# Decoder, experts sublayer: weights added up by transposes, key sums from three engines, all gelus ahead, and the second lane three recurrence states behind

## What is computed

```python
xn = _rmsnorm(x, norm_w)
q = (xn @ w_q.T).reshape(b, t, H, 2, DK)                # H = 8 heads
sim1 = jnp.einsum('bthd,hkd->bthk', q[..., 0, :], keys[:, :, 0, :])   # 32 keys
sim2 = jnp.einsum('bthd,hkd->bthk', q[..., 1, :], keys[:, :, 1, :])
s1, i1 = jax.lax.top_k(sim1, K)                         # K = 8
s2, i2 = jax.lax.top_k(sim2, K)
...
fs, pk = jax.lax.top_k(all_sc, K)                       # of the sums s1 + s2
hidden = jax.nn.gelu(jnp.einsum('btd,bthkd->bthk', xn, wd), approximate=False)
hidden = hidden * jax.nn.relu(fs)
return jnp.einsum('bthk,bthkd->btd', hidden, wu)
```

## Time and profile before

| | us |
|---|---|
| median of 3 runs | 1138.74 (1136.88 to 1139.37) |
| the profiled execution, its own time | 1138.65 |
| span of that execution, first to last instruction | 1136.9 |
| TensorE / VectorE / ScalarE / GpSimd busy | 848.4 / 817.0 / 700.6 / 292.5 |
| mean granted TensorE clock | 0.876 of full |

### The profile page before, as it was taken

The page is one execution under the profiler, slowest core; times in us unless marked ns, Lnnn a source line. Parts: engine busy times, 40 slices in busy tenths (PEclk is TensorE's granted clock), DMA queues, the critical chain, the costliest instruction groups (busy, mean ns, idle before and its releaser), DMA issues. The chain is left out here.

```text
span 1136.9 us, 12090 instructions
## 1 busy us (share of the span) xinstructions
PE 848.4 (75%) x3576; PEld 517.3 (45%) x3576; DVE 817.0 (72%) x1651; ACT 700.6 (62%) x2225; POOL 292.5 (26%) x170
## 2 busy tenths in 40 slices
PE   2657275999977489988976647599996757998883
PEld 1547143555546434354344623455554643435432
DVE  2168763888655689998976875488775559999993
ACT  1412537998378285956852153899748819586590
POOL 0022000888356200000002200188826520000000
PEclk9877576999989699999996758599998969999997
DMA  8100001232000100000000000132200000000000
GB/s 230 38 0 1 1 1 42 89 95 78 1 1 1 33 0 1 0 1 1 1 19 0 1 1 2 45 97 93 65 1 1 1 0 1 1 1 1 1 1 19
DMA packets 26812, 27.37 MB, mean 24 GB/s; under 512 B 7172, under 2 KB 17146, under 8 KB 26746
## 3 DMA queue, kind: packets, MB, share of 16 engines
q1 hardware_dynamic: 24776, 24.63, 7.5%
q10 hardware_dynamic: 1970, 1.97, 0.6%
HBM read 25.28 MB, written 1.31 MB: 23 GB/s over the span
## 5 line engine op out<-in xcount | busy, mean ns | idle before, releaser
L1573 POOL TENSOR_TENSOR rs<-ve,minus_half 128x4 f32<-128x4 f32 (+1 forms) x56 | 89.4, 1596 | 652.7 <-DVE ve L1217 584.3
L963 PE MATMUL ps<-mem,ident 128*128 128x512 f32 x512 | 230.9, 600 | 31.1 <-DVE mem L1542 30.5
L1177 ACT ACTIVATE mem<-mem 128x32 f32<-128x32 f32 x1024 | 217.8, 308 | 0.0
L1593 POOL TENSOR_TENSOR mem<-mem 128x1024 f32<-128x1024 f32 x64 | 150.9, 2361 | 118.3 <-DVE mem L1392 118.1
L1392 DVE TENSOR_TENSOR_SCAN mem<-mem,ps 128x1024 f32<-128x1024 f32 x64 | 145.9, 2285 | 45.2 <-PE ps L799 45.2
L995 ACT ACTIVATE mem<-ps 128x512 f32<-128x512 f32 (+6 forms) x96 | 59.9, 623 | 179.7 <-PE ps L969 59.3
L1542 DVE SCALAR_TENSOR_TENSOR mem<-mem 128x1024 f32<-128x1024 f32 x128 | 159.4, 1279 | 15.3 <-ACT mem L1177 13.8
L963 PEld LDWEIGHTS ps<-mem,ident 128*128 128x128 f32 x512 | 94.1, 190 | 166.8 <-issue 92.3
L806 PE MATMUL ps<-mem,ident 128*128 128x512 f32 x256 | 119.5, 593 | 0.0
L1145 ACT ACTIVATE mem<-ps,mem,rs 128x77 f32<-128x77 f32 x256 | 101.9, 444 | 18.6 <-DVE mem L1445 18.6
L1534 DVE TENSOR_TENSOR mem<-mem 128x1024 f32<-128x1024 f32 x96 | 113.0, 1218 | 0.3
(11 more groups left out here) (221 smaller groups left out, 1221.2 us busy)
## 6 DMA issues: line engine op xcount, KB each, us to landing
mem<-bc_rows SPq DMA_DIRECT2D x64, 256.0 KB, 3.2
mem<-in_x_dram SPq DMA_DIRECT2D x4, 256.0 KB, 3.5
out_dram<-x SPq DMA_DIRECT2D x4, 256.0 KB, 2.3
mem<-in_mask_BxSxS_ik_dram SPq DMA_DIRECT2D x4, 154.0 KB, 3.7
mem<-n_L_ffn_expert_down_dram SPq DMA_DIRECT2D x1, 512.0 KB
mem<-in_L_xattn_Wo_dram SPq DMA_DIRECT2D x1, 512.0 KB
mem<-in_L_xattn_Wv_dram ACTq DMA_DIRECT2D x1, 512.0 KB
a_q<-in_L_xattn_Wq_dram SPq DMA_DIRECT2D x1, 512.0 KB, 4.5
```

Of the source, the lines that this page charges most:

```text
L963: mm = pe.matmul(ps[:, j, :], ident[:], WH[s][:, h % WB, j * 512:(j + 1) * 512], start=(h == 0), stop=(h == PH - 1), skip_group_check=True)
L1177: ins = nc.scalar.activation(SVA[s][:, n % 2, i * NK:(i + 1) * NK], sims[:, 1, h, :], ACT.Identity, bias=sims[:, 0, h, i:i + 1])
L1573: nc.gpsimd.tensor_tensor(RS[s][0:rows, i * n:(i + 1) * n], VE[s][0:rows, i * n:(i + 1) * n], minus_half[0:rows, 0:n], ALU.pow)\
L1593: nc.gpsimd.tensor_tensor(HC[s][:, n % 2], (HS, TU)[n % 2][s][:], spread(CQ[s][:, n % 2, :], 1, DJ), ALU.mult)\
```

## The change

`LAG` becomes 17: in every queue lane 1's instructions stand 17 us of planned time behind lane 0's, and the half-step offsets in cross1 go. The planned times of the other sublayers stay; `PASS` becomes 528.

In the experts, all expert inputs are made transposed (experts down, tokens across, `p_downT` stationary), eight per lane for all 512 tokens, and go through gelu into `GT` before the first weights. A head's weights are added up transposed: eight transposes of 128 x 128 per head that accumulate in PSUM. The product then lies as the last multiplication needs it; its turn and copy go. The key sums of a tile's heads are shared out by `SUMS_BY`: D on VectorE, A on ScalarE, P on TensorE, as a product of the turned similarities (`SIMT`, 64 rows of a head's two halves) with a constant 0/1 pattern `key_pick`, in banks 2 and 3, from where ScalarE copies 1024 columns. Each lane has per tile 3 D, 3 or 4 P and 2 or 1 A. Thresholds get a slack of 2^-20 of the largest absolute key, for which VectorE has a reduction and an operation more. The pattern is made by GpSimd in the setup, stored in DRAM, and loaded once per pass into lane 0's arena. The next pass's x is loaded after two tiles of experts, where it was loaded before their first.

```diff
-    LAG = 0
+    LAG = 17.0
     WB = 4
     XT_TURNS = 6
-    ACT_HEADS = (4, 7)
+    SUMS_BY = [("PDPADPDA", "PDPADPDP"), ("PAPDPADD", "PAPDPDPD")]
+    SLACK = -2.0 ** -20
...
+        GT, WH, HWT, KEY_PICK, SIMT, SUMS, T8, TT, TH, TM = per_lane(
+            gt=(P, (EB, S), F32), wh=(P, (WB, NE), F32), hwT=(P, (EB, P), F32), pick=(P, (NK, NK), F32),
+            simT=(P, (2, PH // 2, P), F32), sums=(P, (PH, NC), F32), t8=(P, (2, PH, TOP), F32),
+            tt=(P, (PH, TOP), F32), th=(P, (2, PH), F32), tm=(P, (PH,), F32))
+        _, SIM = per_lane(front=(P, (11 * DJ * S + S,), F32), sim=(P, (NB, 2 * PH * NK), F32))
+        OS = R
...
+                sp.wait_ge(p_const, 2)
+                sp.dma_start(key_rows.rearrange("p (i j) -> p i j", i=NK), key_made).then_inc(p_hrow, 16)
+                sp.wait_ge(p_hrow, 17)
...
+                w.link(nc.gpsimd.memset(key_made, 0.0))
+                for q in range(4):
+                    ins = nc.gpsimd.affine_select(
+                        out=key_made, in_=key_made, compare_op=ALU.not_equal, fill=1.0, base=-q * NK,
+                        pattern=([[0, NK], [-1, NK]] if q % 2 else [[-1, NK], [0, NK]]), channel_multiplier=1)
+                    if q < 3:
+                        w.link(ins)
+                ins.then_inc(p_const, 1)
...
-            [(0, 344), (3, 352), (10, 357), (18, 397), (30, 402), (38, 442), (50, 447), (58, 487), (70, 492),
-             (78, 532), (90, 539), (94, 541), (95, 545)],
+            [(0, 344), (1000, 1344)],
         ]
-        PASS = 550
+        PASS = 528
+        TILE, HEAD, FIRST = 38.0, 4.75, 16.0
+        pairs = [[(6.5, "keys", 0, 0)] for s in range(LANES)]
+        for s in range(LANES):
+            for k in range(NB):
+                at = FIRST + TILE * k
+                pairs[s] += [(at + HEAD * h - 6, "sum", k, h) for h in range(PH) if SUMS_BY[s][k % 2][h] == "P"]
+                pairs[s] += [(at + TILE + 1.9, "out", k, 0)]
+                if k + 1 < NB:
+                    pairs[s] += [(at + 22, "keys", k + 1, 0)]
+            pairs[s].sort()
+        PAIR = [{use[1:]: n for n, use in enumerate(pairs[s])} for s in range(LANES)]
...
-                                sp.wait_ge(sg["x_ready"][s], (b - 1) * TURNS["x_ready"] + 5)
+                                sp.wait_ge(sg["wh_ready"][s], (b - 1) * TURNS["wh_ready"] + 2 * PH)
...
+                            if s == 0:
+                                yield PASS * b + clock(4, 5)
+                                w.reach(sg["x_ready"][s], 4)
+                                sp.dma_start(key_pick, key_rows.rearrange("p (i j) -> p i j", i=NK)).then_inc(p_toe, 16)
...
+                    def key_sums(k, h):
+
+                        pair("sum", k, h)
+                        if k == 0:
+                            w.reach(G("sim_sb", s), NB)
+                            if s == 0 and h == 0:
+                                pe.wait_ge(p_toe, 48 + 16 * b)
+                        rows = slice(h % 2 * 2 * NK, (h % 2 + 1) * 2 * NK)
+                        for half in range(2):
+                            mm = pe.matmul(ps[:, 2 + half, :], SIMT[s][rows, k % 2, h // 2, :],
+                                           key_pick[rows, half * (NK // 2):(half + 1) * (NK // 2), :]
+                                           .rearrange("p i j -> p (i j)"), start=True, stop=True)
+                        mm.then_inc(G("pair_full", s), 1)
...
+                    def expert_inputs(e):
+
+                        if e < 2:
+                            w.reach(G("sim_sb", s), e + 1)
+                        else:
+                            w.reach(G("g_sb", s), e - 1)
+                        pe.matmul(ps[:, e % 2, :], p_downT[:, e * P:(e + 1) * P], XT[s][:], start=True, stop=True)\
+                            .then_inc(G("z_ready", s), 1)
...
+                        for k in range(NB):
+                            for h in range(PH):
+                                yield FIRST + TILE * k + HEAD * h + 1.6
+                                w.next(G("wh_ready", s))
+                                if h == 0:
+                                    if k == 0:
+                                        w.reach(G("g_sb", s), EB)
+                                    else:
+                                        w.reach(G("hw_ready", s), k)
+                                for e in range(EB):
+                                    mm = pe.matmul(ps[:, e // 4, (e % 4) * P:(e % 4 + 1) * P],
+                                                   WH[s][:, (k * PH + h) % WB, e * P:(e + 1) * P], ident[:],
+                                                   start=(h == 0 and e % 4 == 0), stop=(h == PH - 1 and e % 4 == 3),
+                                                   is_transpose=True, skip_group_check=True)
+                                mm.then_inc(G("wh_used", s), 1)
...
-                        yield 18 + 20 * k
-                        w.next(G("hw_ready", s))
-                        for e in range(EB):
-                            mm = pe.transpose(ps[:, 2 + e // 4, (e % 4) * P:(e % 4 + 1) * P],
-                                              HW[s][:, e * P:(e + 1) * P], ident[:])
-                        mm.then_inc(G("turned", s), 1)
...
+                    def key_sums(k, h):
+
+                        n = k * PH + h
+                        pair("sum", k, h)
+                        if n >= WB:
+                            w.reach(G("wh_used", s), n - WB + 1)
+                        copy(WH[s][:, n % WB, :].rearrange("p (a b) -> p a b", a=2), ps[:, 2:4, :], G("pair_free", s))
...
+                    def own_sums():
+                        for k in range(NB):
+                            sims = SIM[s][:, k, :].rearrange("p (h a n) -> p a h n", a=2, h=PH)
+                            for h in range(PH):
+                                if SUMS_BY[s][k % 2][h] != "A":
+                                    continue
+                                n = k * PH + h
+                                for quarter in range(4):
+                                    yield max(FIRST - 8, FIRST + TILE * k + HEAD * h - 12) + 1.8 * quarter
+                                    if n >= WB and quarter == 0:
+                                        w.reach(G("wh_used", s), n - WB + 1)
+                                    for i in range(quarter * NK // 4, (quarter + 1) * NK // 4):
+                                        ins = nc.scalar.activation(WH[s][:, n % WB, i * NK:(i + 1) * NK],
+                                                                   sims[:, 1, h, :], ACT.Identity,
+                                                                   bias=sims[:, 0, h, i:i + 1])
+                                ins.then_inc(G("asum_ready", s), 1)
...
+                    def others():
+                        for e in range(EB):
+                            yield 7.6 + 0.9 * e
+                            w.next(G("z_ready", s))
+                            nc.scalar.activation(GT[s][:, e, :], ps[:, e % 2, :], ACT.Gelu).then_inc(G("g_sb", s), 1)
...
+                        nc.vector.tensor_reduce(TM[s][:], T8[s][:].rearrange("p a h r -> p h a r"), AX.XY, ALU.max,
+                                                apply_absolute_value=True)
...
+                        th = TH[s][:, k % 2, :]
+                        w.link(nc.vector.scalar_tensor_tensor(out=th, in0=TM[s][:], scalar=SLACK,
+                                                              in1=TT[s][:, :, TOP - 1], op0=ALU.mult, op1=ALU.add))
+                        w.link(nc.vector.tensor_scalar(th, th, 0.0, None, ALU.max))
+
+                    def weighted(k):
+
                         w.reach(G("wh_used", s), (k + 1) * PH)
-                        w.next(G("g_sb", s))
-                        nc.vector.tensor_tensor(HW[s][:], HW[s][:], ps[:, 0:2, :].rearrange("p a b -> p (a b)"),
-                                                ALU.mult).then_inc(G("hw_ready", s), 1)
-                        if k + 1 < NB:
-                            yield 19 + 20 * k
-                            thresholds(k + 1)
-                    yield 94
-                    w.next(G("eo_drained", s), NB)
+                        if k == 0:
+                            w.reach(G("g_sb", s), EB)
+                        else:
+                            w.reach(G("pair_free", s), PAIR[s]["out", k - 1, 0] + 1)
+                        nc.vector.tensor_tensor(
+                            HWT[s], ps[:, 0:2, :].rearrange("p a (b c) -> p (a b) c", c=P),
+                            GT[s][:, :, k * P:(k + 1) * P], ALU.mult).then_inc(G("hw_ready", s), 1)
...
+                    def weights():
+                        for k in range(NB):
+                            for h in range(PH):
+                                n = k * PH + h
+                                wh = WH[s][:, n % WB, :]
+                                yield FIRST + TILE * k + HEAD * h
```

(9 more changed lines are left out.)

262 lines of the change are left out of this document (133 added, 129 removed).

## The result

The changed kernel takes 1220.6 us (1220.3 to 1226.0) beside 1138.8 us for the kernel before: a ratio of 1.073, 95% interval 1.070 to 1.077. The profiled execution has a span of 1224.2 us, 87.3 more than before; it is the longest of four (1226.0 us, the others 1220.3 to 1220.7). The forecast was 1103 us and its range ended at 1140, so both are wrong, and in the wrong direction.

The account below looks back on a forecast made before the run. The experts were taken as bound by VectorE, TensorE close behind. Experts -40, lag +15, borders -14, table loads +4: 1136.9 became 1101.9 us of span, 1103 measured time; forecast 1085 to 1125 (0.52), wider range 1070 to 1140 (about 0.8).

Parts of the forecast that it names:

- The tile: Experts, one tile of both lanes: VectorE 41.1 to 35.0 us, TensorE 38.8 to 35.0; at 92% busy a 38 us tile.
- the prices that I had bounded: Experts' tile: eight accumulating transposes between 1.04 and 1.97 us, taken as 1.06; key reduction plus small operation 0.5 per lane.
- The start of the stage: Start of the experts: twelve more expert inputs and gelus, partly hidden in free time, cost 4 us per batch (0 to 10.8).
- -40: Experts in all: tiles -21.9, start +4, end -2, together -19.9 us per batch, -40 over both.
- The lag, "paid once, at the very end": Whole kernel: lane 1 running 17 us behind costs +15 us (12 to 17), only once, at the end.
- what an overlap gives back: Borders between stages: half the neighbouring busy times added, fullest engine taken; ceiling 20.3 us, 14 taken as gain.
- third rival: Lanes block each other in the queues: stages before the experts +25 us per batch, 1168 us (cases 1141 to 1168); chance 0.11.
- two signs: What would show lanes blocking each other before the experts: recurrence states over 5.9 us or a front over 110.
- The table loads: Recurrence: the lagging lane's exp and logarithm switches need two more loads per batch, +4 us in all (0 to 5).
- The moved loads and the setup: Next x and pattern loads arrive well before use; setup work runs beside ScalarE's: nothing, some 6 us without that cover.
- The clock: TensorE in the experts' tiles: by the trace the clock stays at 2.4 GHz despite transposes; by the skill's rule 1.2 GHz.
- fourth rival: Clock falls in the experts' tiles: TensorE 35 becomes 66 us a tile, 184 us more, about 1330 us; chance 0.02.

Follow-up runs that it names:

- The runs with four own heads: Changed kernel, lane 1 late only in the experts' tiles, each lane's first four key sums on VectorE: 1144.4 us, lag 12 1156.7; ScalarE's head later, inputs and gelus closer 1131.3.
- the nested runs: Changed kernel with the lag starting ever earlier, always to the experts' end: from the experts 1172.7 us, from cross1 1185.1, from the scan 1210.7; everywhere 1220.6.
- the fastest kernel: Changed kernel, lag 17 only in the experts' tiles, first four key sums on VectorE, ScalarE's head one place later, inputs and gelus closer: 1131.3 us, ratio 0.993.
- the one with three engines: Changed kernel with its lag taken out (LAG = 0, cross1's half step back), key sums still shared over VectorE, ScalarE and TensorE: 1178.6 us, ratio 1.035.

## Why the prediction was wrong

*The tile: right, step by step.* VectorE 35.0 was forecast, 35.3 measured; TensorE 35.0 and 33.7; the cycle 38, 38.4 in the mean, at 92% of VectorE. ScalarE was low by 3.3 (29.2, 32.5 measured) and covered. Groups of the kernel after, 431 to 612 us (busy us, mean ns), with the prices that I had bounded:

```profile
L1043 PE MATMUL ps<-ident,mem 128*128 128x128 f32 x496 | 65.4, 284 | 11.4 <-DVE mem L1671 11.3
...
L1623 DVE TENSOR_REDUCE mem<-mem 128x8 f32<-128x128 f32 x7 | 2.0, 286 | 0.2
L1629 DVE SCALAR_TENSOR_TENSOR mem<-mem 128x8 f32<-128x8 f32 x8 | 1.4, 173 | 0.3
```

The small operations are 0.29 + 0.17 for the 0.50 assumed per lane. Eight accumulating transposes take 1.04 us at the full clock (row at 452.76 of the timeline; 1.06 assumed). What I didn't see is that the 38 us need the lag: side by side the same instructions make tiles of 44.2. I had put the gain of the tiles and the lag into the sum as two terms that don't touch, so the 38 was right by luck in part.

*The start of the stage: the step that failed first.* I charged it 4 us a batch, by free time of the engines (0 to 10.8), and "four weight buffers let VectorE go ahead". They didn't: the first heads were given to TensorE and ScalarE, whose queues hold 16 inputs and 16 gelus there. It measured +19 side by side and +23 to +31 with the lag. Free time was the wrong measure, twice over. The added inputs and gelus weren't hidden (11.3 us with the sums divided as before), and where the first heads stand in the queues cost 7.9 more. The runs with four own heads show the second part from the other side: with five instead of three of the first tile's heads on VectorE, and lane 1 late only from there on, the start is 57.0. Hence the experts were +22.5 us in two passes, not -40, and some +16 by estimate (twice the 8.0 of pass 1) in an execution whose two passes are alike.

*The lag, "paid once, at the very end": half right.* Lane 1 ends 14.3 us after lane 0 (12 to 17 forecast). But each border costs as well. I took half of the neighbouring busy times for what an overlap gives back (14 us). They give nothing and cost 48, as the nested runs show, and 12.3 more at the border out of the experts, where I had 3.3 as the most to be gained. So the sum missed the span by 122.3 us: 62.5 in the experts, 62.1 in the stages before them (52.1 for -14 + 4), and -2.3 at the end. This is the third rival's mechanism in its main point, that lanes block each other in the queues, and its 25 us per batch before the experts was well sized (22.3 and 29.8 measured). Where it looked for them is another matter: of its two signs, states over 5.9 us didn't come and a front over 110 did in pass 2 (114.7), and 29.8 of the 52.1 us are in cross1, which it didn't name. Its total of 1168 failed on the -40, which I had kept in it: 1136.9 + 22.5 + 52.1 + 12.7 = 1224.2. I gave it 0.11 because I asked only what the steady states do under a lag. That was zero, as I said (ten scans take 28.2 us after, as before in the middle of the stage), though it holds for a lag of three whole states and not for one and a half. The borders I had only tested for busy time.

*The table loads: right.* Four more, 5.1 us; both switches of the recurrence are there four times instead of twice:

```profile
L1150 ACT ACT_TABLE_LOAD x4 | 5.1, 1283 | 0.1
L1159 ACT ACT_TABLE_LOAD x4 | 5.1, 1283 | 0.1
```

*The moved loads and the setup: right.* The setup's last work ends at 42.1 us instead of 41.4, and the longer list of waits names a DMA only within the setup.

*The clock: the rows were right.* In the full tile, with sixteen times eight transposes, the granted clock is 1.00. The fourth rival doesn't happen. The rule of the Trainium skill ("TensorE: Matmul & The Clock Gate", Part 4: PE-mode transpose) that transposes don't engage the full clock is contradicted by the earlier trace rows, where TensorE had hardly anything but transposes at 0.51 and the clock then stood at 0.99; this tile doesn't test it, since the heads' transposes are 16.2 of its 33.7 busy us and the rest are matmuls of other kinds. The clock falls elsewhere, in the starts and at the borders (0.77, 0.70).

## What to carry to other kernels

Where engines take their work in a fixed order, price an added operation by what stands behind it in its queue and who waits for that, not by the engine's free time. An engine that is moved off the critical work for balance must keep it at the start of a stage, until the others have caught up: here the first four heads on VectorE, with one more exchange in the order, took 8 us off the start of each pass. A lag between lanes pays in the stage whose order is made for it, and opening and closing it costs as well, since a lane alone is bound by its own chain: open it in as few stages as possible, and count the border behind the last one.

## What was not expected of the hardware

One thing, and it is of the queues and the clock together. Four key-sum matmuls take 1.98 us at the full clock and 3.78 at the low one, and the low one comes in the very 45 us in which the engines wait for one another (granted clock 0.77). Where most of those waits are gone the clock is high again. Windows of the fastest kernel, from its first key sum to its first weighted product:

```profile
408.80:444.60 35.80, 32.57 (x145) 19.90 (x144) 30.43 (x61) 26.12 (x82) 0.00 (x0) 0.95 0.00 1
```

Over its whole span the mean granted clock is 0.884 in this execution of 1127.2 us and 0.869 in the three of 1131.3 to 1132.0; over that of the changed kernel it is 0.845. The mean by itself doesn't rank kernels: with the sums divided as before, side by side, it is 0.817, and that kernel is 22 us faster than the one with three engines at 0.853.

That the clock is a cause and not only a sign can be seen in the two passes of the changed kernel, which have the same instructions in the same order. Counted from the stage's x, they agree within 0.1 us until a low stretch of the clock, which lasts from 46.6 to 56.9 us in pass 1 and from 46.5 to 60.2 in pass 2. The low clock then comes back in pass 2 alone, from 73.9 to 87.5 us. The same key sums on TensorE, 72.3 us after the x in pass 1 and 73.8 in pass 2:

```profile
483.85 1.98 PE L996 MATMUL ps<-mem 64*128 64x512 f32 x4
...
1058.90 3.78 PE L996 MATMUL ps<-mem 64*128 64x512 f32 x4
```

The first weighted product comes 7.7 us later for it, and the stage ends 6.5 us later. Why the clock fell in one pass and not in the other stays open. How much of the other losses at the starts and borders is the clock's, and how much the waits', no run separates.
